# The first steps of a software pipeline: q and k projected ahead of v, and the weights loaded by thirds

## The reference

```python
x = x + conv(ln_c(x), Wq, Wk, Wv, Wb, Wo)          # conv(t) = t + delta_rule(...) @ Wo
t = tokens(x)
x = t + ffn(ln_t(t))                               # 8 experts, top 2, and a shared expert
...
q = l2norm(heads(silu(t @ Wq)))                    # 12 heads of 16
k = l2norm(heads(silu(t @ Wk)))
v = heads(silu(t @ Wv))
beta = sigmoid(t @ Wb)
# per head, for each token in order:
#   u = beta * (v - S^T k);  S = S + k u^T;  o = S^T q
...
g, u = silu(x @ w_gate), x @ w_up                  # each expert, 192 wide; the shared one 768
expert = (g * u) @ w_down
```

## Time and profile before

| | |
|---|---|
| median of the runs | 491.64 us (491.04 to 492.1) |
| the profiled run, and its span | 491.26 us, 489.3 us |
| PE busy | 414.9 us, 85% |
| DVE busy | 416.6 us, 85% |
| ACT busy | 345.4 us, 71% |
| POOL busy | 412.1 us, 84% |
| DMA over the span | 44.10 MB, 90 GB/s |

### The profile page before, as it was taken

The page is one execution under the profiler, slowest core; times in us unless marked ns, Lnnn a source line. Parts: engine busy times, 40 slices in busy tenths (PEclk is TensorE's granted clock), DMA queues, the critical chain, the costliest instruction groups (busy, mean ns, idle before and its releaser), DMA issues.

```text
span 489.3 us, 10450 instructions
## 1 busy us (share of the span) xinstructions
PE 414.9 (85%) x2400; PEld 382.5 (78%) x2400; DVE 416.6 (85%) x2290; ACT 345.4 (71%) x1023; POOL 412.1 (84%) x527
## 2 busy tenths in 40 slices
PE   1514254899999999999999999999999989999996
PEld 0403132789899999999898989898989889898895
DVE  4208999999999999999999999999999999996200
ACT  3539455587887878796969696969786848485862
POOL 5319989899999999999999999999999999986340
PEclk9755665799999999999999999999999999999998
DMA  7967344453233232323233222322333232300301
GB/s 201 223 135 170 89 109 106 115 128 100 72 91 80 80 89 70 100 70 90 82 83 88 83 90 78 96 68 69 99 85 88 76 91 73 103 1 1 114 1 16
DMA packets 45213, 44.10 MB, mean 90 GB/s; under 512 B 20384, under 2 KB 36960, under 8 KB 45152
## 3 DMA queue, kind: packets, MB, share of 16 engines
q1 hardware_dynamic: 43680, 42.84, 34.1%
q10 hardware_dynamic: 1472, 0.60, 0.5%
HBM read 37.13 MB, written 6.29 MB: 89 GB/s over the span
## 4 chain that ended last, share of the span: by engine, by line
DVE 47%; PE 23%; ACT 10%; POOL 8%; issue 8%; DMA 2%; ACTq 1%; POOLq 0%; SPq 0%; DVEq 0%
DVE Pr L1365 11%; DVE bank L1369 10%; DVE u L1367 9%; DVE SH L1373 8%; PE bank L447 5%; ACT L724 3%; POOL PQ L923 3%; POOL PQ L916 2%; PE bank L420 2%; PE bank L432 2%; PE bank L424 2%; PE bank L422 2%; PE bank L423 2%; PE bank L421 2%; POOL hid L961 2%
## 5 line engine op out<-in xcount | busy, mean ns | idle before, releaser
L961 POOL TENSOR_TENSOR hid<-sg,ug 128x192 f32<-128x192 f32 x192 | 112.7, 607 | 22.8 <-ACT ug L690 19.3
L916 POOL TENSOR_TENSOR PQ<-SH,QB 128x768 f32<-128x768 f32 x62 | 112.7, 1840 | 1.8 <-DVE SH L1373 1.8
L923 POOL TENSOR_TENSOR PQ<-PQ 128x768 f32<-128x768 f32 (+2 forms) x93 | 103.0, 1107 | 6.1
L447 PE MATMUL bank<-Wd,hidT 128*128 128x192 f32 x576 | 106.6, 326 | 0.0
L689 ACT ACTIVATE sg<-bank 128x192 f32<-128x192 f32 x192 | 63.5, 331 | 58.4 <-PE bank L424 48.3
L1369 DVE TENSOR_TENSOR bank<-bank,u 128x96 f32<-128x96 f32 (+1 forms) x467 | 104.2, 264 | 0.1
L1367 DVE TENSOR_REDUCE u<-Pr 128x6 f32<-128x102 f32 (+1 forms) x437 | 102.3, 268 | 0.6 <-issue 0.2
L1365 DVE TENSOR_TENSOR Pr<-SH,bank 128x96 f32<-128x96 f32 (+1 forms) x437 | 100.8, 265 | 2.2 <-DVE negmax L1203 0.3
L1373 DVE TENSOR_TENSOR SH<-SH,bank 128x96 f32<-128x96 f32 (+1 forms) x467 | 101.7, 255 | 0.3
L447 PEld LDWEIGHTS bank<-Wd,hidT 128*128 128x128 f32 x576 | 94.5, 190 | 0.0
L420 PE MATMUL bank<-Whi,hiT 128*128 128x384 f32 (+1 forms) x192 | 73.5, 383 | 1.3 <-DVE loT L1121 1.1
(11 more groups left out here) (146 smaller groups left out, 797.5 us busy)
## 6 DMA issues: line engine op xcount, KB each, us to landing
QB<-q_scratch SPq DMA_DIRECT2D x64, 384.0 KB
k_scratch<-khl SPq DMA_DIRECT2D x60, 48.0 KB, 1.7
KR<-k_scratch SPq DMA_DIRECT2D x30, 96.0 KB, 2.4
q_scratch<-qn SPq DMA_DIRECT2D x64, 24.0 KB, 1.6
Wd<-in_L_ffn_w_down_dram SPq DMA_DIRECT2D x4, 288.0 KB, 8.0
out_dram<-xT SPq DMA_DIRECT2D x1, 896.0 KB, 4.1
Wlo_unsplit<-in_L_ffn_w_gate_dram SPq DMA_DIRECT2D x1, 768.0 KB, 5.3
Wlo_unsplit<-in_L_ffn_w_up_dram SPq DMA_DIRECT2D x1, 768.0 KB, 7.7
```

The source lines that it names most:

```text
L447: last = mm(bDn[:, 0:C], hidT[:, turn_half(g), k - lo, :], Wd[:, k, :], start=False, stop=(k == KT - 1))
L916: tt(PQ[:, at * BR * HP:(at + n) * BR * HP].rearrange("p (i b h) d -> p i b (h d)", i=n, b=BR), SH[:, lo:lo + n].rearrange("p i b h d -> p ...
L923: chained(tt(PQ[:, :, 0:w], PQ[:, :, 0:w], PQ[:, :, w:2 * w], ALU.add))
L961: tt(hid[:, r * H:(r + 1) * H], sg[:, m % RING], ug[:, m % RING], ALU.mult).then_inc(s_hid, 1)
```

## The change

In the steps below 1 TensorE does `A_qk` ahead of `A_vb`, and ScalarE's `A_silu_v` moves behind `A_sq`. The copy `A_khi` of chunk 0 moves from step -1 to the end of the scales in step -2, and GpSimd's `A_kn` and `A_klo` of chunk 0 move ahead of the work there. SyncE issues the first k, as it does the others: it waits for k after issuing all of `raw0`, the router columns and the first third of `raw1`; behind k and q come the second third, the spreading of q and the last third. Every third of a tile has its own semaphore, and `weights_hi0` and `weights_hi1` wait for the third that they need. The rows 128 to 191 come from memory once, into partitions 64 to 127; each `weights_hi1` copies them to partitions 0 to 63 on ScalarE. The clearing of `Wpz` on GpSimd goes ahead of that of the spare tiles, with its own semaphore.

```diff
--- before.py
+++ after.py
@@ -134,7 +134,7 @@
             "weights_hi_ready", "weights_lo0_ready", "weights_1_ready", "zeros_ready"))
         s_split, s_low0 = sem("tokens_split"), sem("low_rows_zero")
         s_wp, s_wo, s_wr, s_wd = (sem(n) for n in ("wp_in", "wo_in", "wr_in", "wd_in"))
-        s_wu = [sem("up_weights0_in"), sem("up_weights1_in")]
+        s_wu0, s_wu1 = ([sem(f"up_weights{i}_{g}_in") for g in range(3)] for i in range(2))
         s_x = [sem("x_first_in"), sem("x_rest_in")]
         s_hlo, s_wps = sem("h_low_ready"), sem("projection_weights_split")
         s_const, s_zero, s_id, s_low = sem("consts_ready"), sem("state_zero"), sem("ident_ready"), sem("lower_ready")
@@ -144,6 +144,7 @@
         s_act = sem("act_chain")
         s_xs, s_xT, s_nm1, s_h, s_xh = (sem(n) for n in ("xs_ready", "xT_ready", "nmr1_ready", "h_ready", "xh_ready"))
         s_x1 = sem("x1_ready")
+        s_wpz = sem("projection_zeros_ready")
         s_plus = sem("one_plus_rstd_ready")
         s_ve1, s_ve2, s_rs = sem("variance1_ready"), sem("variance2_ready"), sem("rstds_ready")
         s_hTp, s_hT, s_qk, s_vb, s_z, s_qks, s_vs, s_sq, s_ss, s_inv = (sem(n) for n in (
@@ -209,18 +210,19 @@
 
             return bKB[slot // 8 % 2][:, 2 * BR * G + lo:2 * BR * G + lo + n]
 
-        def load_up(eng, i, to, lo, hi):
-
-            units = to[:, R:].rearrange("p (u w) -> p u w", u=UN)
+        def load_up(eng, g, ready, to, lo, hi):
+
+            n = UN // 3
+            units = to[:, R:].rearrange("p (u w) -> p u w", u=UN)[:, g * n:(g + 1) * n]
             for half, we, ws in ((0, w_gate, ws_gate), (H, w_up, ws_up)):
-                eng.dma_start(units[:, 0:E, half:half + H], we[:, lo:hi, :].rearrange("e c h -> c e h")).then_inc(s_wu[i], 16)
-                eng.dma_start(units[:, E:UN, half:half + H], ws[lo:hi, :].rearrange("c (s h) -> c s h", h=H)).then_inc(s_wu[i], 16)
-
-        def load_router(eng, i, to, lo, hi):
-
-            eng.dma_start(to[:, 0:E], router_w[lo:hi, :]).then_inc(s_wu[i], 16)
+                src = we[g * n:(g + 1) * n, lo:hi, :].rearrange("e c h -> c e h") if g < 2 else ws[lo:hi, :].rearrange("c (s h) -> c s h", h=H)
+                eng.dma_start(units[:, :, half:half + H], src).then_inc(ready[g], 16)
+
+        def load_router(eng, ready, to, lo, hi):
+
+            eng.dma_start(to[:, 0:E], router_w[lo:hi, :]).then_inc(ready[0], 16)
             for at in range(E, R):
-                eng.dma_start(to[:, at:at + 1], sg_w[lo:hi, :]).then_inc(s_wu[i], 16)
+                eng.dma_start(to[:, at:at + 1], sg_w[lo:hi, :]).then_inc(ready[0], 16)
 
         def load_projection(eng, w, lo, hi):
 
@@ -280,12 +282,17 @@
                 load_x(0, 0, FIRST * T)
                 load_projection(sp, Wq, 0, C)
                 load_projection(sp, Wk, C, 2 * C)
-                load_up(sp, 0, raw0, 0, C0)
-                load_router(sp, 0, raw0[:, :], 0, C0)
-                load_up(sp, 1, raw1[0:C1], C0, C)
-                load_up(sp, 1, raw1[C1:P], C0, C)
-                load_router(sp, 1, raw1[0:C1], C0, C)
-                load_router(sp, 1, raw1[C1:P], C0, C)
+                load_router(sp, s_wu0, raw0[:, :], 0, C0)
+                for g in range(3):
+                    load_up(sp, g, s_wu0, raw0, 0, C0)
+                load_router(sp, s_wu1, raw1[C1:P], C0, C)
+                load_up(sp, 0, s_wu1, raw1[C1:P], C0, C)
+                scratch_k(sp, 0, 0)
+                load_k(sp, 0, 0)
+                scratch_q(0, 0)
+                load_up(sp, 1, s_wu1, raw1[C1:P], C0, C)
+                spread_q(0, 0)
+                load_up(sp, 2, s_wu1, raw1[C1:P], C0, C)
                 sp.dma_start(Wo0[:, :], Wo[0:C0, :]).then_inc(s_wo, 16)
                 sp.dma_start(Wo1[:, :], Wo[C0:C, :]).then_inc(s_wo, 16)
                 sp.dma_start(sgb[:, :], sg_b.rearrange("(a n) -> a n", a=1).to_broadcast([P, 1])).then_inc(s_wr, 16)
@@ -309,8 +316,8 @@
                 if c >= 0:
                     at(1, partial(scratch_k, sp))
                     at(1, partial(load_k, sp))
-                at(1, scratch_q)
-                at(1, spread_q)
+                    at(1, scratch_q)
+                    at(1, spread_q)
                 if c == -1:
                     load_later()
                 for i in range(KT // 3):
@@ -464,8 +471,8 @@
                     at(1, fill, 1)
                     at(3, A_h)
                     at(1, fill, 2)
+                    at(3, A_qk)
                     at(3, A_vb)
-                    at(3, A_qk)
                 elif c < NC:
                     at(-2, Fb_up, 5)
                     at(0, fill, 3)
@@ -665,17 +672,19 @@
 
             def weights_hi0(m):
 
+                if m % (UN // 3) == 0:
+                    act.wait_ge(s_wu0[m * 3 // UN], (2 if m else 3 + R - E) * 16)
+                f(Whi0[:, columns(m)], raw0[:, columns(m)], ACT.Copy).then_inc(s_whi, 1)
+
+            def weights_hi1(m):
+
                 if m == 0:
-                    act.wait_ge(s_wu[0], 7 * 16)
-                f(Whi0[:, columns(m)], raw0[:, columns(m)], ACT.Copy).then_inc(s_whi, 1)
-
-            def weights_hi1(m):
-
-                if m == 0:
-                    act.wait_ge(s_wu[1], 14 * 16)
-                    act.wait_ge(s_clear, len(free) + 1)
+                    act.wait_ge(s_clear, len(free))
+                if m % (UN // 3) == 0:
+                    act.wait_ge(s_wu1[m * 3 // UN], (2 if m else 3 + R - E) * 16)
                 if m >= len(free):
                     act.wait_ge(s_w1, m - len(free) + 1)
+                f(raw1[0:C1, columns(m)], raw1[C1:P, columns(m)], ACT.Copy)
                 f(spare(m)[C1:P].bitcast(F32R), raw1[C1:P, columns(m)], ACT.Copy).then_inc(s_whi, 1)
 
             def unit(q, p, m):
@@ -726,16 +735,12 @@
 
                 at = partial(stage, c, par)
                 if c < 1:
-                    at(1, A_khi)
-                    once(c, -1, scratch_k, act, 0, 0)
-                    once(c, -1, load_k, act, 0, 0)
+                    if c >= 0:
+                        at(1, A_khi)
                     at(3, A_xs)
                     once(c, -1, weights_hi0, 2)
                     once(c, 0, weights_hi1, 2)
                     once(c, -1, weights_hi0, 3)
-                    if 0 <= c + 2 < NC:
-                        table(0, SILU)
-                    at(2, A_silu_v)
                     once(c, 0, weights_hi1, 3)
                     once(c, 0, weights_hi1, 4)
                     at(0, place, 1)
@@ -744,8 +749,10 @@
                     at(2, A_silu_qk)
                     once(c, -1, weights_hi0, 4)
                     at(2, A_sq)
+                    at(2, A_silu_v)
                     table(c + 2, LN_EXP)
                     at(2, A_inv)
+                    once(c, -2, A_khi, 0, 0)
                     at(3, A_plus)
                     at(1, place, 0)
                     once(c, 0, weights_hi1, 5)
@@ -969,9 +976,12 @@
                         rsqrt(c)
                     at(0, reading, 0)
                     once(c, -1, weights_lo0, 4)
+                    once(c, -2, A_kn, 0, 0)
                     at(2, A_vn)
                     once(c, 0, weights_1, 5)
-                    at(2, A_kn)
+                    if c > -2:
+                        at(2, A_kn)
+                    once(c, -2, A_klo, 0, 0)
                     once(c, -1, weights_lo0, 5)
                     once(c, -1, weights_lo0, 6)
                     once(c, -1, weights_lo0, 7)
@@ -986,7 +996,8 @@
                     once(c, -1, weights_1, 2)
                     once(c, 0, weights_1, 6)
                     once(c, -1, weights_lo0, 9)
-                    at(2, A_klo)
+                    if c > -2:
+                        at(2, A_klo)
                     once(c, 0, weights_1, 7)
                     once(c, -1, weights_lo0, 10)
                     once(c, -1, weights_1, 3)
@@ -1048,9 +1059,9 @@
             pool.affine_select(out=lower[:, :, :], in_=lower[:, :, :], compare_op=ALU.is_gt, fill=0.0, base=0,
                                pattern=[[1, E], [-1, E]], channel_multiplier=0).then_inc(s_low, 1)
             pool.memset(SH[:, T - 1], 0.0).then_inc(s_zero, 1)
+            pool.memset(Wpz[:, :], 0.0).then_inc(s_wpz, 1)
             for b in free:
                 pool.memset(b, 0.0).then_inc(s_clear, 1)
-            pool.memset(Wpz[:, :], 0.0).then_inc(s_clear, 1)
             pool.memset(loT[:, :, :].bitcast(F32), 0.0).then_inc(s_low0, 1)
             pool.memset(hlo[:, :].bitcast(F32), 0.0).then_inc(s_low0, 1)
             pool.wait_ge(s_const, 4)
@@ -1141,7 +1152,7 @@
             def split_projections():
 
                 dve.wait_ge(s_wp, 12 * 16)
-                dve.wait_ge(s_clear, len(free) + 1)
+                dve.wait_ge(s_wpz, 1)
                 w0 = count(nc.vector.tensor_copy(Wphi0[:, :], Wp0[:, :]))
                 w1 = count(nc.vector.tensor_copy(Wpz[C1:P].bitcast(F32R), Wp1[C1:P, :]))
                 dve.wait_ge(*w0)
```

## The result

The changed kernel takes 487.9 us in the median of five runs (486.9 to 488.7), the kernel before 491.6; the ratio is 0.9929, 95% interval 0.9915 to 0.9943. The profiled run took 487.5, its span 485.6, against 491.26 and 489.3. So 3.7 us of the 4.5 forecast arrived, inside the range of 484.8 to 489.4.

The account below looks back on a forecast made before the run. The DVE recurrence bounds the middle, ScalarE's stop on the first k the start. 7.9 us gained before the scan less 3.4 lost in step 0 leaves 4.5: 486.8 profiled, 487.0 us forecast, range 484.8 to 489.4.

Parts of the forecast that it names:

- ScalarE stopped by its own DMA: At the start, ScalarE issues the first k and stops 10.1 us; freed, it takes up `A_xs(2)` 9.0 us earlier.
- Steps -2 and -1: Before the scan: `A_xs(2)` at 22.95, `inv(1)` at 30.2, scan start at 31.6 (8.1 earlier), `hhi` of tokens 2 at 36.3.
- k by SyncE is not waited for: Before the scan: SyncE issues k at 21.25, it finds empty queues and lands at 28.2, with no wait by the fills.
- The wait of 1.5 us for beta: Step 0, DVE slot 17: v and beta projected behind q and k end 1.5 us later, so DVE idles ahead of `zc`.
- The loss in step 0: Step 0: four extra copies of 0.43 us and the later silu of v delay `A_stats(3)` at slot 24 by 3.4 us.
- No further loss behind slot 24: From slot 24 of step 0 on, every row stays 4.5 us earlier than in the kernel before.
- The sum: Whole run: profiled 491.26 minus 4.5 gives 486.8; the median is 0.4 above it, stated as 487.0 us.
- that ScalarE is not what holds step 0: Rival, step 0: only the projection swap costs, 1.5 us at slot 17, so 6.4 us gained and 485.1 us; chance 0.14.
- the cover of step 1: Rival, steps 0 and 1: slack of ScalarE or GpSimd gone, five copies and late v cost 2.1 more, 489.1 us; chance 0.16.
- Late weights: Rival, step 0: the middle third of the last rows lands 6.2 us after ScalarE's unit 4 wants it, 493.2 us; chance 0.04.

Follow-up runs that it names:

- experiment 4: The changed kernel with the first k issued by ScalarE again, at the start of step -1: 491.9 us, ratio 1.0012.
- experiment 1: The kernel before with SyncE instead of ScalarE issuing the first k, behind all the weights: 489.7 us, ratio 0.9961.
- experiment 3: The changed kernel with the last 64 rows loaded twice by DMA again and no extra copies on ScalarE: 491.2 us, ratio 0.9996.
- 6: The changed kernel with all thirds of the last rows issued ahead of the first k: 487.7 us, ratio 0.9925.
- experiment 2: The changed kernel with v and beta projected ahead of q and k again, silu of v where it was before: 485.8 us, ratio 0.9902.
- 11: The changed kernel with v first, tokens 8 to 15 of x loaded in step 2, last rows loaded twice and no extra copies: 486.5 us.
- experiment 5: The changed kernel with one more 64 x 384 copy on ScalarE for each of units 1 to 4: 490.0 us, ratio 0.9967.
- 7: The changed kernel with tokens 8 to 15 of x loaded only in step 1, ahead of the last down weights: 491.1 us, ratio 0.9985.
- 10: The changed kernel with tokens 8 to 15 of x loaded only in step 2, behind the down weights: 487.7 us, ratio 0.9924.
- 8: The changed kernel with v projected first and tokens 8 to 15 of x loaded only in step 1: 487.0 us, ratio 0.9903.
- 9: The changed kernel with v projected first and tokens 8 to 15 of x loaded in step 2, behind the down weights: 484.0 us, ratio 0.9849.
- Experiment 12: The changed kernel with the two row copies of units 3 and 4 in a row, then the two roundings: 487.8 us, a single run.

## Why the prediction was right, and where it was not

- *ScalarE stopped by its own DMA*: right. 9.1 us at `A_xs(2)` against 9.0, and giving the stop back in experiment 4 takes the whole gain. Taking it away alone is not enough: in experiment 1, with the last rows still loaded twice, that gave 1.5 us. The second k took most of it back there, as it took all of it in experiment 3, which loads them twice with the rest of the change in place.
- *Steps -2 and -1*: right to 0.1. `A_xs(2)` at 22.84 (22.95), `inv(1)` at 30.13 (30.2), scan at 31.56 (31.6), `hhi` of tokens 2 at 36.33 (36.3).
- *k by SyncE is not waited for*: right; its reading was issued at 24.11 where I had 25.2. By the ring order that the Trainium skill's page "DMA: Bandwidth & Descriptors" gives, section on queues, rings and completion order, k would have waited behind what stood ahead of it. No run contradicts that order: in 6 the first k had 0.79 MB more ahead of it and lost 0.6 us, and the second k, behind the rest of x, lost 4.3. A queue of its own was no protection: in 4 the reading of the first k, on ScalarE's queue, took up to 10.4 us to land, where it took 2.3 to 2.6 on SyncE's in the changed kernel.
- *The wait of 1.5 us for beta*: right, 1.47.
- *The loss in step 0*: mechanism right, size too small. The term was 4 x 0.43 for the extra copies, from a pair of like instructions. A copy and a rounding by turns don't overlap, so a unit takes 1.07 and not 0.86, and the four take 4.3 us where they took 2.0: they add 2.3, not 1.7. Three neighbours that overlapped before no longer do (the last `hhi` copy and `xs`, each now followed by a copy, and `place`, now followed by the table load), 0.1 us each. Together that is 0.9 over the 1.7 of the term, and the loss is as much over the forecast: DVE waited 2.69 where I had 1.9, and the loss was 4.31 against 3.4. That lies outside the 2.4 to 3.8 that I gave as its bounds: I had taken the duration of one instruction as the most that a copy could cost, and forgot that it also stops its neighbour's overlap. `hhi` of tokens 2 reached DVE 7.86 earlier (36.36 against 44.22), and 7.86 - 4.31 = 3.55, which is what the clock of the scan shows.
- *No further loss behind slot 24*: right, but by luck. I followed each transfer to its own user, x to `A_xs(4)`, and did not ask which transfers stand behind it on SyncE. The second k does. It had some 2.5 us of room before the scan would have waited (see the result), which the prediction never worked out. The unnamed rival, a second k that is late, made DVE wait 3.6, 3.6, 6.4 and 2.8 us in experiments 1, 2, 3 and 11.
- *The sum*: the profiled run's 486.8 and the 0.4 by which the median lies higher make 487.1 to 487.2, and not 487.0.
- *The rivals*: that ScalarE is not what holds step 0 fell with experiment 5; the cover of step 1 held. Late weights were not seen: TensorE, DVE and GpSimd wait for no weights, and ScalarE starts unit 4 without a gap.

## What to carry to other kernels

A DMA that depends on another DMA is issued from an engine with nothing else to do: the compute engine that issues it stops until the first has landed. Here that was 10 us, or 4 where the write met little traffic. When work is moved earlier, the next transfer on the same queue can become the limit before the next engine does, as the second k did here; list for every bulk load what is queued behind it and when that is wanted. And of two projections into banks that are reused, the one whose bank the next chunk needs goes first; with its silu placed to match, that was 3.7 us here.

## What the runs showed that I had not expected

- ScalarE's instructions overlap by about 0.1 us in some pairs and not in others: 64-partition copies by turns with roundings come 0.53 apart, two of a kind 0.42 to 0.43. It isn't likeness as such: in the kernel before, the rounding of a weight unit and the writing of h overlap too, 0.42 apart.

```profile
39.53 0.51 ACT L670 ACTIVATE Whi<-Wlo_unsplit 128x384 fp32r<-128x384 f32 x1
39.95 0.49 ACT L561 ACTIVATE h<-bank,nmr,rs 128x192 f32<-128x192 f32 x1
```

  These rows fit the rule that both must have the same first partition of input and output (0 for both in this pair; the copy writes partition 0 and the rounding 64). Experiment 12 doesn't separate this from other differences of the two, such as the type written.
- From step 1 to step 2 the profiled runs take either 25.6 us (before, changed, 3, 6, 7, 10) or 26.5 (1, 2, 4, 5, 8, 9, 11, 12). It goes with TensorE's pace at the first Wo matmuls. The first pair of these, in the changed kernel and in experiment 5, and what DVE then does in the latter:

```profile
69.41 0.56 PE L407 MATMUL bank<-xh,ident 128*128 128x192 f32 x2
```

```profile
71.55 1.01 PE L407 MATMUL bank<-xh,ident 128*128 128x192 f32 x2
```

```profile
74.17 0.37 DVE L1106 BATCH_NORM_STATS2 st<-bank 128x6 f32<-128x192 f32 x1 [0.83 <-PE bank L409]
```

  In the first, TensorE has a short spell at the pace of 2.4 GHz just there, in the second it stays at that of 1.2, and DVE waits 0.8 us for the result. The same wait of 0.83 stands in all the runs that take 26.5 and in none that take 25.6. Which of the two a run gets may explain part of the spread of the changed kernel's runs (486.9 to 488.7), but not the 2.8 us within those of experiment 2; that is a guess from profiled runs alone, and what starts the spell is open. The windows of granted clock don't settle it: in experiment 5 they show 1.00 all through the start, while 384-column matmuls start 0.32 us apart there (13.00, 13.32, 13.64), 1.2 columns a ns. They do so too in the kernel before at 46.71 and 47.03, where the window from 43 to 49 shows 0.50, and start 0.17 to 0.18 apart from 142.6 to 144.4, some 2.2 columns a ns, where it shows 1.00.
